# The offset filters of a channel gate: from three small matmuls on TensorE to three running sums on VectorE

## Time and profile before

| | us |
|---|---|
| median of 3 runs | 1666.94 (1665.14 to 1667.64) |
| the profiled execution, its own time | 1666.51 |
| its span, first to last instruction | 1664.8 |
| PE busy | 1594.8 (96%) |
| DVE busy | 1245.4 (75%) |
| ACT busy | 1177.7 (71%) |
| POOL busy | 792.6 (48%) |

### The profile page before, as it was taken

One profiled execution on the slowest core, in us unless ns is written; L12 is line 12 of the kernel. 1 busy time (PEld: TensorE's weight loads), 2 busy tenths in 40 slices (PEclk: granted clock), 3 DMA queues, 4 the chain that ended last, 5 costly groups with the idle time before them and its releaser, 6 DMA issues.

```text
span 1664.8 us, 36807 instructions
## 1 busy us (share of the span) xinstructions
PE 1594.8 (96%) x10439; PEld 1331.8 (80%) x10439; DVE 1245.4 (75%) x4518; ACT 1177.7 (71%) x3044; POOL 792.6 (48%) x1759
## 2 busy tenths in 40 slices
PE   1799999999999999999999999999999999999998
PEld 1588888888888888888888888888888888888887
DVE  5477777777777777777777777777777777777675
ACT  2477677777677777677777777777777777777775
POOL 4554454454454455554454554454554454554430
PEclk9999999999999999999999999999999999999999
DMA  3134443444444444443444434344434344434233
GB/s 122 34 103 128 144 114 119 129 107 127 145 110 123 127 108 128 145 109 124 124 109 130 145 106 127 119 114 130 145 104 129 114 119 130 145 100 133 74 85 121
DMA packets 73558, 197.68 MB, mean 119 GB/s; under 512 B 11536, under 2 KB 52880, under 8 KB 65168
## 3 DMA queue, kind: packets, MB, share of 16 engines
q1 hardware_dynamic: 73360, 195.32, 40.1%
HBM read 51.62 MB, written 51.38 MB: 62 GB/s over the span
## 4 chain that ended last, share of the span: by engine, by line
PE 68%; POOL 18%; issue 7%; DVE 5%; ACT 2%; POOLq 0%; DVEq 0%; ACTq 0%
PE ps_s L384 16%; PE ps_o L417 15%; PE ps_v L451 10%; PE ps_p L434 9%; PE ps_t L396 7%; PE ps_p L429 6%; POOL hats L704 4%; POOL hats L703 2%; ACT hats L610 2%; DVE e L905 1%; POOL yb_row L744 1%; POOL xb_diag L745 1%; POOL hat_sum L706 1%; PE ps_v L477 1%; POOL g L685 1%
## 5 line engine op out<-in xcount | busy, mean ns | idle before, releaser
L549 ACT ACTIVATE e<-e,zmin 128x256 f32<-128x256 f32 x800 | 404.2, 505 | 258.5 <-DVE zmin L905 254.8
L417 PEld LDWEIGHTS ps_o<-eT,v 128*128 128x128 f32 x3584 | 478.1, 192 | 70.8 <-issue 69.8
L417 PE MATMUL ps_o<-eT,v 128*128 128x128 f32 (+1 forms) x3584 | 518.5, 272 | 0.4 <-ACT eT L564 0.4
L905 DVE CUSTOM_DVE_ANT_0 e<-ps_s,mask 128x256 f32<-128x256 f32 x800 | 334.6, 418 | 224.9 <-PE ps_s L384 216.9
L384 PE MATMUL ps_s<-kk,qq 128*128 128x256 f32 x1408 | 436.2, 392 | 2.1 <-DVE zmin L905 2.1
L918 DVE TENSOR_SCALAR e<-e,rz 128x256 f32<-128x256 f32 x800 | 361.2, 452 | 0.0
L564 ACT ACTIVATE eT<-ps_t 128x512 f32<-128x512 f32 (+1 forms) x416 | 235.9, 567 | 107.6 <-PE ps_t L396 103.4
L396 PE MATMUL ps_t<-ident,e 128*128 128x128 f32 x1600 | 305.7, 273 | 0.0
L396 PEld LDWEIGHTS ps_t<-ident,e 128*128 128x128 f32 x1600 | 225.2, 141 | 80.5 <-issue 0.2
L451 PE MATMUL ps_v<-wvox,xb 128*128 128x128 f32 x2048 | 272.4, 276 | 1.6 <-DVE v L937 1.4
L451 PEld LDWEIGHTS ps_v<-wvox,xb 128*128 128x128 f32 x2048 | 253.0, 193 | 15.8 <-issue 14.2
(11 more groups left out here) (154 smaller groups left out, 1636.9 us busy)
## 6 DMA issues: line engine op xcount, KB each, us to landing
raw<-in_x_dram SPq DMA_DIRECT2D x32, 1568.0 KB, 8.7
out_dram<-raw SPq DMA_DIRECT2D x32, 1568.0 KB, 5.4
v<-v SPq DMA_DIRECT2D x192, 256.0 KB, 3.7
kk<-kk SPq DMA_DIRECT2D x192, 112.0 KB, 2.2
ksp<-kk SPq DMA_DIRECT2D x192, 64.0 KB, 2.6
kk<-kk SPq DMA_DIRECT2D x32, 224.0 KB, 2.9
w_s<-in_w_dram SPq DMA_DIRECT2D x1, 64.0 KB, 6.4
wv_s<-in_wv_dram SPq DMA_DIRECT2D x1, 64.0 KB, 5.3
```

The source lines that it names most:

```text
L417: last = nc.tensor.matmul(o[:, UPIX * max(0, c - 1):UPIX * min(UNITS, c + 1)], v[:, s, c, :], eT[:, UPIX * (base + a):UPIX * (base + b)], ...
L549: nc.scalar.activation(e[:, i, :], e[:, i, :], ACT.Exp, bias=zmin[:, i:i + 1], scale=-1.0, accum_out=zs[:, i:i + 1]).then_inc(e_done.next( ...
L905: nc.vector.tensor_tensor_reduce(e[:, i, :], ps_s[(TILES * n.parity() + t) % 2][:, 0:KEYS], mask[:].rearrange("p s h a b -> p (s h a b)"), ...
```

## The change

The three matmuls of c3 go. TensorE only makes the broadcast row (`ones x diag`). `conv` is built with its band turned round, so that row i of `conv[:, k, :]` holds the three taps that output channel i needs. VectorE then copies the row first, and makes each offset as a product of the row with `conv[:, k, :]` with a running sum over the 128 columns (`accum_out`). The add of the base positions and the clip follow. A wait for ScalarE's last use of the position columns, one image earlier, is added. The product's elementwise output goes to `cells`, a buffer used only at the start. The step numbers that other engines wait for move up by three. No DMA is changed.

```diff
-CHAIN_READS = ((2, "d1"), (4, "d3"), (7, "d4"), (11, "d9"), (13, "d11"), (16, "d13"))
-N_DG, N_PG, N_CG, N_AG = 16, 33 + 4 + 9, 6, 4
+CHAIN_READS = ((2, "d1"), (4, "d3"), (5, "d4"), (14, "d9"), (16, "d11"), (19, "d13"))
+N_DG, N_PG, N_CG, N_AG = 19, 33 + 4 + 9, 6, 4
...
                         if at == CH["c3"]:
                             pe.wait_ge(pg.sem, pg.count(m, 7))
-                            for k in range(TAPS):
-                                nc.tensor.matmul(ps_v[:, 4 + k:5 + k], conv[:, k, :], col(PL), start=True, stop=True)
                             nc.tensor.matmul(ps_v[:, 8:8 + P], ones[:], diag[:], start=True, stop=True).then_inc(cg.next(), 1)
...
                             if at == CH["a4"]:
 
-                                act.wait_ge(dg.sem, dg.count(m, 6))
+                                act.wait_ge(dg.sem, dg.count(m, 10))
...
                         if at == CH["d4"]:
                             dve.wait_ge(cg.sem, cg.count(m, 3))
-                            step(5, nc.vector.tensor_tensor(col(POS, 3), ps_v[:, 4:7], base_f[:], ALU.add))
-                            step(6, nc.vector.tensor_scalar(col(POS, 3), col(POS, 3), 0.0, P - 1.0, ALU.max, ALU.min))
-                            step(7, nc.vector.tensor_copy(pooled_row[:], ps_v[:, 8:8 + P]))
+                            step(5, nc.vector.tensor_copy(pooled_row[:], ps_v[:, 8:8 + P]))
+                            dve.wait_ge(ag.sem, ag.count(m + -1, 3))
+                            for k in range(TAPS):
+                                nc.vector.scalar_tensor_tensor(cells[:, k, 0:P], pooled_row[:], 1.0, conv[:, k, :], ALU.mult, ALU.mult,
+                                                               accum_out=col(POS + k)).then_inc(dg.next(), 1)
+                            dve.wait_ge(dg.sem, dg.count(m, 8))
+                            step(9, nc.vector.tensor_tensor(col(POS, 3), col(POS, 3), base_f[:], ALU.add))
+                            step(10, nc.vector.tensor_scalar(col(POS, 3), col(POS, 3), 0.0, P - 1.0, ALU.max, ALU.min))
```

More of the change, by code:

```diff
@@ L424, in hidden @@
                         if g == 0:
-                            pe.wait_ge(dg.sem, dg.count(m, 14))
+                            pe.wait_ge(dg.sem, dg.count(m, 17))
                             pe.wait_ge(pg.sem, pg.count(m, 37))
@@ L482, in chain @@
                         if at == CH["c5"]:
-                            avg(5, col(SQ1), 12, 3)
+                            avg(5, col(SQ1), 15, 3)
                         if at == CH["c6"]:
@@ L612, in slot @@
                             if at == CH["a6"]:
-                                act.wait_ge(dg.sem, dg.count(m, 8))
+                                act.wait_ge(dg.sem, dg.count(m, 11))
                                 nc.scalar.activation(col(EX), col(ZS), ACT.Exp, bias=nbd[:, 0:1],
@@ L708, in chain @@
                         if at == CH["p7"]:
-                            gp.wait_ge(dg.sem, dg.count(m, 10))
+                            gp.wait_ge(dg.sem, dg.count(m, 13))
                             gp.wait_ge(o_done.sem, o_done.count(m + -4, STRIPS))
@@ L724, in chain @@
                         if at == CH["p9"]:
-                            gp.wait_ge(dg.sem, dg.count(m, 11))
+                            gp.wait_ge(dg.sem, dg.count(m, 14))
                             steps(23,
@@ L732, in chain @@
                         if at == CH["p11"]:
-                            gp.wait_ge(dg.sem, dg.count(m, 13))
+                            gp.wait_ge(dg.sem, dg.count(m, 16))
                             steps(26, *rsqrt(col(R1), col(VE1), col(T0)),
@@ L750, in chain @@
                             if c == 0:
-                                gp.wait_ge(dg.sem, dg.count(m, 16))
+                                gp.wait_ge(dg.sem, dg.count(m, 19))
                                 gp.wait_ge(v_done.sem, v_done.count(m + -2, 2 * PAIRS))
@@ L881, in tables @@
                             for k in range(TAPS):
-                                nc.vector.tensor_scalar(conv[:, k, :], band[:, 0, :], wg_s[:, 3 * k:3 * k + 1], None,
+                                nc.vector.tensor_scalar(conv[:, k, :], band[:, TAPS - 1, :], wg_s[:, 3 * k:3 * k + 1], None,
                                                         ALU.mult).then_inc(v_w, 1)
@@ L886, in tables @@
                                 for k in range(TAPS):
-                                    nc.vector.scalar_tensor_tensor(conv[:, k, :], band[:, j, :],
+                                    nc.vector.scalar_tensor_tensor(conv[:, k, :], band[:, TAPS - 1 - j, :],
                                                                    wg_s[:, 3 * k + j:3 * k + j + 1], conv[:, k, :],
@@ L968, in chain @@
                             dve.wait_ge(cg.sem, cg.count(m, 3))
-                            step(5, nc.vector.tensor_tensor(col(POS, 3), ps_v[:, 4:7], base_f[:], ALU.add))
-                            step(6, nc.vector.tensor_scalar(col(POS, 3), col(POS, 3), 0.0, P - 1.0, ALU.max, ALU.min))
-                            step(7, nc.vector.tensor_copy(pooled_row[:], ps_v[:, 8:8 + P]))
+                            step(5, nc.vector.tensor_copy(pooled_row[:], ps_v[:, 8:8 + P]))
[6 more added lines that the diff above has]
+                            step(10, nc.vector.tensor_scalar(col(POS, 3), col(POS, 3), 0.0, P - 1.0, ALU.max, ALU.min))
                         if at == CH["d6"]:
                             dve.wait_ge(pg.sem, pg.count(m, 15))
-                            step(8, nc.vector.scalar_tensor_tensor(junk[:], pooled_row[:], 1.0, hat_sum[:],
+                            step(11, nc.vector.scalar_tensor_tensor(junk[:], pooled_row[:], 1.0, hat_sum[:],
                                                                    ALU.mult, ALU.mult, accum_out=col(ZS)))
@@ L977, in chain @@
                             dve.wait_ge(ag.sem, ag.count(m, 4))
-                            step(9, nc.vector.tensor_scalar(col(EX), col(EX), 1.0, None, ALU.add))
-                            step(10, nc.vector.reciprocal(col(GATE), col(EX)))
+                            step(12, nc.vector.tensor_scalar(col(EX), col(EX), 1.0, None, ALU.add))
+                            step(13, nc.vector.reciprocal(col(GATE), col(EX)))
                         if at == CH["d9"]:
                             dve.wait_ge(cg.sem, cg.count(m, 4))
-                            step(11, nc.vector.tensor_tensor(col(D1), col(M1), ps_v[:, 2:3], ALU.subtract))
+                            step(14, nc.vector.tensor_tensor(col(D1), col(M1), ps_v[:, 2:3], ALU.subtract))
                             dve.wait_ge(pg.sem, pg.count(m, 23))
-                            step(12, nc.vector.scalar_tensor_tensor(col(SQ1), col(D1), col(D1), col(AV),
+                            step(15, nc.vector.scalar_tensor_tensor(col(SQ1), col(D1), col(D1), col(AV),
                                                                     ALU.mult, ALU.add))
@@ L987, in chain @@
                             dve.wait_ge(cg.sem, cg.count(m, 5))
-                            step(13, nc.vector.tensor_scalar(col(VE1), ps_v[:, 3:4], EPS, None, ALU.add))
+                            step(16, nc.vector.tensor_scalar(col(VE1), ps_v[:, 3:4], EPS, None, ALU.add))
                         if at == CH["d13"]:
@@ L992, in chain @@
                             dve.wait_ge(pg.sem, pg.count(m + -1, N_PG))
-                            step(14, nc.vector.tensor_tensor(b1x[:, m.parity():m.parity() + 1], ps_v[:, 0:1],
+                            step(17, nc.vector.tensor_tensor(b1x[:, m.parity():m.parity() + 1], ps_v[:, 0:1],
                                                              bn_t[:, 0:1], ALU.add))
-                            step(15, nc.vector.tensor_tensor(d_row[:], ps_v[:, P:2 * P], wobv[:], ALU.add))
-                            step(16, nc.vector.tensor_copy(r_row[:], ps_v[:, 2 * P:3 * P]))
+                            step(18, nc.vector.tensor_tensor(d_row[:], ps_v[:, P:2 * P], wobv[:], ALU.add))
+                            step(19, nc.vector.tensor_copy(r_row[:], ps_v[:, 2 * P:3 * P]))
                     def slot(n, t):
```

## The result

| | median us | runs |
|---|---|---|
| before | 1667.29 | 1665.14 to 1669.38, 4 runs |
| after | 1651.86 | 1651.49 to 1652.63, 4 runs |

A forecast was written before the change was run, and what follows sets the result against it. TensorE was taken as bound until slot 21, then the hat chain to L434 of slot 27. Per image -0.67 + 0.28 = -0.39 us, over 30 images -11.7: from 1666.94 to 1655 us, range 1647 to 1665.

The forecast's parts named there:

- the part given back: VectorE's delay beyond the slack at tile 21's exponential, returning at L434 of slot 27: 0.28 us per image.
- What bounds: TensorE hands over near slot 21 to ScalarE, POOL's hats, VectorE's sum, then `hid` and L434 of slot 27, idle 0.56 us.
- TensorE saves 0.67 us per image: Six weight loads of L477 in slot 19 removed, 0.112 us each, all of it on the path.
- c: Distance between starts of successive products on VectorE in slot 20: 0.25 us, own range 0.22 to 0.33.
- D: VectorE's delay of the piece after d4 in slot 20: 0.39 + 2c, 0.89 us (0.83 to 1.19).
- Slack 0.61: Tile 21's exponential could start at 809.76 but starts at 810.37, ScalarE being busy with keys and queries: 0.61 us hidden.
- The first two images count 0: No attention there: 0.67 us or more less on TensorE against 0.89 more on VectorE, counted as 0.
- Nothing given back: Rival: VectorE's delay stays under 0.61 us, or L434 does not wait for the hats: 1646.8 us, chance 0.11.
- All given back: Rival: each product waits for the previous read-out, 0.40 us apart; 0.58 us given back per image: 1664.2 us, chance 0.19.
- VectorE the bound: Rival: VectorE bounds slots 20 to 27, products 0.70 us apart, 1.58 us given back per image: 1694 us, chance 0.13.
- half throughput: Skill rule for the products' two float32 SBUF sources: distance about 0.40 us; forecast said the before trace doesn't bear it out.

The follow-up runs named there:

- e7: Kernel after, with the third hat's two POOL instructions and the last add of hat_sum cut to one column: 1630.70 us, ratio to before 0.9785.
- e6: Kernel after, with one bn_stats moved behind the mask, interpolated sum and gate's exponential from slot 24 to 25, d7 and p7 from 25 to 26: 1631.32 us.
- e3: Kernel before without the three one-column matmuls, VectorE unchanged, pooled-row columns standing in for the offsets: 1645.69 us, ratio to before 0.9875.
- e1: Kernel after, with one bn_stats piece on VectorE moved from slot 20 to slot 21, behind the mask of tile 21: 1646.17 us, ratio to before 0.9877.
- e2: Kernel after, with the three one-column matmuls put back on TensorE as dead work: 1672.12 us, ratio to before 1.0033.
- e5: Kernel after, with a dead 128x384 SBUF copy on POOL in slot 20, beside the three products: 1656.72 us, ratio to before 0.9942.

## Why the prediction was right

The measured 1651.9 lies in the stated range, but under the 1653 to 1660 that went with the forecast alone: the mechanism was right, and the part given back was about half of what was forecast.

- *What bounds.* The hand-over from TensorE at slot 21 to hats, sum, `hid` and L434 of slot 27 was read rightly: e7 shortens the hat chain alone and gains 21 us. It was also right that `hid` and not p7 releases L434: in e6 p7 comes a slot later, its fifth instruction ends at 802.27, and L434 starts at 801.52 without a wait.
- *TensorE saves 0.67 us per image.* Measured 0.68 in e3's period.
- *The products' distance c = 0.25, VectorE's delay D = 0.89.* c was 0.21 to 0.22, at or under the lower end of its range: a read-out delays nothing. Two distances make 0.07 us of D. The first product started 0.32 us after the start of the row copy, not 0.37, which is another 0.05; the rest took what was forecast, to 0.01. Together D = 0.76. This is the term that was mis-sized.
- *Slack 0.61.* The exponential waits 0.18 us and comes 0.15 later than its place behind the queries before; L434 of slot 27 comes 0.15 later too: 0.76 - 0.61 = 0.15. The given-back part, forecast 0.28, was half of that; 30 x 0.13 = 3.9 us is about the difference between the forecast -11.7 and the measured -15.
- *The first two images count 0.* At L434 of slot 27 in the second image's chain both kernels stand together (70.11 and 70.10 us from the start). In the third image's, the first of the 30, the kernel after is 0.65 us ahead (120.37 instead of 121.02).
- *The rivals.* "Nothing given back" falls with e1, e2 and e3. "All given back" needed c = 0.40. "VectorE the bound" needed products of 0.67 us: e5 shows that such a length comes with a POOL copy beside them, and slot 20 has none. The Trainium skill (SBUF — State Buffer, section SBUF: two separate sides) states a lock on the port pair that VectorE and GpSimd share, held for the whole instruction; e5 agrees, as the product that met the copy was held to about the copy's end. The half throughput that the Trainium skill states for two float32 sources in SBUF (Vector Engine (DVE) Microarchitecture Reference, section Points that are easy to get wrong) does not show: products 0.21 apart stand beside copies 0.20 apart.

## What to carry to other kernels

Work moved from the busiest engine to one with room is paid for in the place where it lands: find the next reader behind it in that queue, measure that reader's slack, and count only the excess. If an independent piece stands between the moved work and that reader, put it behind the reader (e1), and the excess is gone. And where a strictly ordered engine stands at a wait for a slow side chain, look one slot further: asking for the result later (e6) was worth as much here as the whole change.

## What the runs showed that I had not expected

- Products with a running sum start 0.21 us apart, where plain copies start 0.20 apart, though each record is 0.29 us and its read-out 0.08 more.
- A float32 matmul that moves one column costs TensorE 0.22 us, two weight-load records of 0.112 us (e3: 0.68 us for three).
- A product of two SBUF tiles of 128x128 takes 0.28 us alone and 0.58 to 0.67 beside a POOL copy; the same hat instruction on POOL takes 0.71 us, and 0.85 us when it starts 0.08 us behind VectorE's scaling.
